# First loads cut into pieces in the order of use, and conditioned weight chunks awaited in halves

## What is computed

```python
w = weight[adapter_ids]
h = jnp.einsum('bsi,boi->bso', x, w)              # the conditioned product

gu_s = x2 @ shared_w_gate_up.T                    # x2 is h, as (2048, 1024)
shared_out = jax.nn.silu(g_s) * u_s @ shared_w_down.T
probs = jax.nn.softmax(x2 @ gate_w.T, axis=-1)
topk_vals, topk_idx = jax.lax.top_k(probs, 2)     # then normalised
gu = jnp.einsum('th,eih->eti', x2, w_gate_up)
out_e = jnp.einsum('eti,ehi->eth', jax.nn.silu(g) * u, w_down)
return x + moe_out + shared_out
```

## Time and profile before

| | |
|---|---|
| median of 3 runs | 1063.91 us (1063.42 to 1065.25) |
| the profiled execution | 1064.86 us, span 1063.1 us |
| TensorE matmul busy | 1055.3 us (99%), 4826 matmuls |
| VectorE busy | 634.1 us (60%) |
| ScalarE busy | 457.0 us (43%) |
| GpSimd busy | 272.8 us (26%) |
| DMA | 248.03 MB, mean 233 GB/s |
| granted TensorE clock | 1.000 over the span |

### The profile page before, as it was taken

The page is one execution under the profiler, slowest core; times in us unless marked ns, Lnnn a source line. Parts: engine busy times, 40 slices in busy tenths (PEclk is TensorE's granted clock), DMA queues, the critical chain, the costliest instruction groups (busy, mean ns, idle before and its releaser), DMA issues.

```text
span 1063.1 us, 15851 instructions
## 1 busy us (share of the span) xinstructions
PE 1055.3 (99%) x4826; PEld 870.8 (82%) x4827; DVE 634.1 (60%) x650; ACT 457.0 (43%) x527; POOL 272.8 (26%) x325
## 2 busy tenths in 40 slices
PE   8999999999999999999999999999999999999998
PEld 7888888888888888887888888888888888888887
DVE  6666765536756667867866867354553545544454
ACT  6565644532223556756655755232223222322310
POOL 1000000000026655555555550121003200033040
PEclk9999999999999999999999999999999999999999
DMA  9899877422256779987987865663566336564355
GB/s 351 325 348 342 315 286 258 190 79 81 88 209 211 263 273 348 335 313 270 352 351 265 291 248 213 246 229 119 145 232 237 138 118 182 194 237 144 113 183 211
DMA packets 55350, 248.03 MB, mean 233 GB/s; under 512 B 8146, under 2 KB 21586, under 8 KB 45394
## 3 DMA queue, kind: packets, MB, share of 16 engines
q1 hardware_dynamic: 29394, 161.50, 42.0%
q0 software_dynamic: 19008, 62.41, 17.0%
q10 hardware_dynamic: 6912, 23.66, 5.9%
HBM read 200.87 MB, written 43.52 MB: 230 GB/s over the span
## 4 chain that ended last, share of the span: by engine, by line
PE 98%; DMA 1%; issue 1%; DVE 0%; ACT 0%; SPq 0%; ACTq 0%; DVEq 0%
PE bank L568 32%; PE bank L570 32%; PE bank L569 32%; PE bank L593 1%; PE bank L779 1%; DMA raw<-cond_w 0%; ACT w_split_sb L863 0%; PE bank L581 0%; PE bank L712 0%; PE bank L602 0%; DVE w_split_sb L1157 0%; DMA ids<-ids 0%; PE bank L699 0%; PE bank L747 0%; DVE rows L1413 0%
## 5 line engine op out<-in xcount | busy, mean ns | idle before, releaser
L1157 DVE TENSOR_TENSOR w_split_sb<-raw,w_split_sb 128x2048 fp32r<-128x2048 f32 (+3 forms) x152 | 257.3, 1724 | 60.0 <-ACT w_split_sb L863 58.8
L863 ACT ACTIVATE w_split_sb<-raw 128x2048 fp32r<-128x2048 f32 (+3 forms) x152 | 215.7, 1456 | 63.7 <-PE bank L570 53.5
L507 POOL DMA_INDIRECT h_in<-h_dram,idx_h x156 | 175.5, 1125 | 122.6 <-DVE tile_f L1462 75.1
L568 PE MATMUL bank<-hT_hi,w_split_sb 128*128 128x512 f32 x512 | 199.7, 390 | 0.0
L569 PE MATMUL bank<-hT_lo,w_split_sb 128*128 128x512 f32 x512 | 199.2, 389 | 0.0
L570 PE MATMUL bank<-hT_hi,w_split_sb 128*128 128x512 f32 x512 | 199.2, 389 | 0.0
L568 PE MATMUL bank<-w_split_sb,tile_hT 128*128 (+1 forms) x312 | 124.8, 400 | 0.0
L570 PE MATMUL bank<-w_split_sb,tile_hT 128*128 (+1 forms) x312 | 122.0, 391 | 0.0
L569 PE MATMUL bank<-w_split_sb,tile_hT 128*128 (+1 forms) x312 | 121.7, 390 | 0.0
L570 PEld LDWEIGHTS bank<-hT_hi,w_split_sb 128*128 128x128 f32 x512 | 96.1, 188 | 20.0
L568 PEld LDWEIGHTS bank<-hT_hi,w_split_sb 128*128 128x128 f32 x512 | 96.1, 188 | 19.9
(11 more groups left out here) (153 smaller groups left out, 1417.0 us busy)
## 6 DMA issues: line engine op xcount, KB each, us to landing
raw<-sh_gu_w SPq DMA_DIRECT2D x16, 2048.0 KB, 9.3
raw<-exp_gu_w SPq DMA_DIRECT2D x16, 2048.0 KB
raw<-cond_w SPq DMA_DIRECT2D x14, 2048.0 KB, 9.8
y_dram<-y_out ACTq DMA_DIRECT2D x39, 512.0 KB
raw<-sh_down_w SPq DMA_DIRECT2D x8, 2048.0 KB, 7.7
raw<-exp_down_w SPq DMA_DIRECT2D x16, 1024.0 KB
h_dram<-h_blk POOLq DMA_DIRECT2D x16, 512.0 KB, 8.8
x_raw_sb<-xT SPq DMA_DIRECT2D x7, 1024.0 KB, 9.6
```

The lines of the kernel that those rows point to most:

```text
L507: nc.gpsimd.indirect_dma_start(out=h_in[par][:, i, :], out_offset=None, in_=h_blocks, in_offset=bass.IndirectOffsetOnAxis(ap=idx_h[par][:, ...
L568: nc.tensor.matmul(dst, lhs[0], rhs[0], start=first, stop=False)
L863: return nc.scalar.activation(dst, src, ACT.Copy)
L1157: return nc.vector.tensor_tensor(dst, src, hi.bitcast(F32), ALU.subtract)
```

## The change

It has these parts.
- ScalarE's queue issues two of the four x pieces at the start, the third after the copy of the first, the fourth after the copy of the first w piece. The gate weights are loaded after the last w piece's copy, and their copy and subtraction stand at unit 4.
- ScalarE and VectorE take one x piece (two k), then its two w pieces, and so on. Each x piece has a signal of its own for TensorE (`first_x_split`).
- TensorE does both token tiles per k of the first chunk (`first_batch`), in banks 2 and 3, then the second chunk's units in banks 0 and 1, awaited by quarters (`second_split`).
- SP loads the third chunk in quarters, each when its part of the raw buffer has been split; ScalarE and VectorE split it, and TensorE awaits it, by quarters.
- TensorE awaits each later conditioned chunk in two halves (`w_begun` ahead of k = 0, `w_split` ahead of k = 4).
- 7 x 9 dummy matmuls instead of 8 x 9.

The core of the diff (semaphore declarations, starting values and repeated forms are left out):

```diff
+            def x_load(b):
+                sp.wait_ge(x_split, b + 1)
+                sp.dma_start(x_raw_sb[:, :], xT[bass.ds(b, 1), :, :].rearrange("o p n -> (o p) n")).then_inc(x_in, 16)
+
+            def first_loads():
...
+                x_load(1)
+                a = sp.value_load(small["ids"][0:1, 1:2], min_val=0, max_val=ADAPTERS - 1)
+                for i, landed in enumerate(third_w):
+                    c0, c1 = i * CH // 4, (i + 1) * CH // 4
+                    if i < 3:
+                        sp.wait_ge(first_split, 2 * i + 2)
+                    else:
+                        sp.wait_ge(w_split, 3)
+                    sp.dma_start(raw[0][:, c0:c1], cond_w[bass.ds(a, 1), 0, :, c0:c1].rearrange("o p n -> (o p) n")).then_inc(landed, 16)
+                chunk(3, 1, cond_w[bass.ds(a, 1), 1, :, :].rearrange("o p n -> (o p) n"))
...
+            def first_batch():
+
+                for k in range(KT):
+                    if k == KT - PIECE_K:
+                        pe.wait_ge(x_split, 2)
+                    elif k % PIECE_K == 0:
+                        pe.wait_ge(first_x_split, k // PIECE_K + 1)
+                    if k < KT - 1:
+                        pe.wait_ge(first_split, k + 1)
+                    else:
+                        pe.wait_ge(w_split, 3)
+                    for m in range(2):
+                        last = first_product(bank[2 + m][:, :], 0, m, k)
+                        if k == KT - 1:
+                            last.then_inc(h_mm, 1)
+                for m in range(2):
+                    for k in range(KT):
+                        if m == 0 and k == KT - 2:
+                            pe.wait_ge(w_split, 4)
+                        elif m == 0 and k % 2 == 0:
+                            pe.wait_ge(second_split, k // 2 + 1)
+                        last = first_product(bank[m][:, :], 1, m, k)
+                    last.then_inc(h_mm, 1)
...
-                        if not first or b2 or n:
-                            pe.wait_ge(w_split, 4 * q + 2 * b2 + n + 3)
+                        third = first and b2 == 1 and n == 0
+                        if not third:
+                            pe.wait_ge(w_begun, 4 * q + 2 * b2 + n - 2)
...
+                                if m == 0 and third and k % 2 == 0 and k < KT - 2:
+                                    pe.wait_ge(third_split, k // 2 + 1)
+                                if m == 0 and k == (KT - 2 if third else KT // 2):
+                                    pe.wait_ge(w_split, 4 * q + 2 * b2 + n + 3)
...
-            with pe.Fori(0, 8):
+            with pe.Fori(0, 7):
...
+            for i in range(2):
+                first_x_load(i)
...
+                if i == 0:
+                    first_x_load(2)
+                for k in (2 * i, 2 * i + 1):
+                    act.wait_ge(first_w[k], 16)
+                    copy(w_split_sb[:, 0, 0, k * HALF:(k + 1) * HALF], raw[0][:, k * HALF:(k + 1) * HALF]).then_inc(first_hi, 1)
+                    if k == 0:
+                        first_x_load(3)
...
+            def w_hi_third():
+                act.wait_ge(h_mm, 4)
+                for i, landed in enumerate(third_w):
+                    act.wait_ge(landed, 16)
+                    copy(w_split_sb[:, 0, 0, i * CH // 4:(i + 1) * CH // 4], raw[0][:, i * CH // 4:(i + 1) * CH // 4]).then_inc(third_hi, 1)
...
+                    if first and u == 1:
+                        x_hi_part(1, 1)
```

More of the change, by code:

```diff
@@ L178, in adaln_ffn_kernel @@
         second_w = [sem(f"second_w{i}") for i in range(4)]
+        third_w = [sem(f"third_w{i}") for i in range(4)]
         second_hi = sem("second_hi")
+        second_split = sem("second_split")
+        third_hi = sem("third_hi")
+        third_split = sem("third_split")
+        w_begun = sem("w_begun")
         first_hi = sem("first_hi")
+        first_x_split = sem("first_x_split")
         first_split = sem("first_split")
@@ L315, in _ @@
             sp.sem_inc(x_in, 16)
-            sp.sem_inc(raw_in[0], 16)
+            sp.sem_inc(raw_in[0], 32)
             sp.sem_inc(raw_in[1], 16)
@@ L336, in cond_loads @@
+            def cond_loads(q):
                 for b2 in range(2):
                     b = 2 * q + b2
[L338 to L346, removed]
@@ L351, in cond_loads @@
                         chunk(4 * q + 2 * b2 + n, n, cond_w[bass.ds(a, 1), n, :, :].rearrange("o p n -> (o p) n"))
-                        if n == 0 and not first:
+                        if n == 0:
                             move(2 * q - 2 + b2, b2)
-            cond_loads(0, first=True)
+            first_loads()
             with sp.Fori(1, QUARTERS) as q:
@@ L604, in transpose_logits, with first_product @@
                 last.then_inc(lt_mm, 1)
+            def first_product(dst, n, m, k):
+                return product(dst, [x_split_sb[0][:, hl, k, m * P:(m + 1) * P] for hl in range(2)],
+                               w_cols(n, k, 0, HALF), k == 0, k == KT - 1)
+            def first_batch():
[20 more added lines that the diff above has]
+                    last.then_inc(h_mm, 1)
             def cond_quarter(q, first=False, ends=False):
                 for b2 in range(2):
-                    if not first or b2:
-                        pe.wait_ge(x_split, 2 * q + b2 + 2)
+                    if first and b2 == 0:
+                        first_batch()
+                        continue
+                    pe.wait_ge(x_split, 2 * q + b2 + 2)
                     for n in range(2):
-                        if not first or b2 or n:
-                            pe.wait_ge(w_split, 4 * q + 2 * b2 + n + 3)
+                        third = first and b2 == 1 and n == 0
+                        if not third:
+                            pe.wait_ge(w_begun, 4 * q + 2 * b2 + n - 2)
                         for m in range(2):
@@ L849, in _, with first_x_load @@
         def _(act):
-            for i in range(PIECES):
+            def first_x_load(i):
                 act.dma_start(x_raw_sb[:, i * PIECE_K * SEQ:(i + 1) * PIECE_K * SEQ],
                               xT[0, :, i * PIECE_K * SEQ:(i + 1) * PIECE_K * SEQ]).then_inc(first_x[i], 16)
-            act.dma_start(small["gate_raw"][:, :, :], gate_w).then_inc(gate_in, 16)
-            act.sem_inc(w_hi, 4)
+            for i in range(2):
+                first_x_load(i)
+            act.sem_inc(w_hi, 6)
             act.sem_inc(x_hi, 1)
@@ L916, in cond_quarter @@
                         w_hi_second()
+                    elif first and u == 2:
+                        w_hi_third()
                     elif m == 0:
@@ L920, in cond_quarter @@
                             w_hi_half(c, (n + 1) % 2, hf, (h_mm, 2 * c, 16 * (2 * q + b2 + (1 if n == 0 else 2))))
-                    if n == 0 and m == 1 and not (last and b2 == 1):
+                    if n == 0 and m == 1 and not (last and b2 == 1) and not (first and b2 == 0):
                         act.wait_ge(h_mm, UPQ * q + 4 * b2 + 2)
                         x_hi_part(2 * q + b2 + 1, 1 - b2)
+                    if first and u == 4:
+                        gate_hi()
                     if u == 6 and last:
```

69 lines of the change are left out of this document (37 added, 32 removed).

## The result

| | kernel before | changed kernel |
|---|---|---|
| median (lowest to highest, 22 runs each) | 1063.96 us (1063.05 to 1065.82) | 1062.68 us (1062.13 to 1063.46) |
| ratio, 95% interval | | 0.9988 (0.9982 to 0.9993) |
| the profiled execution, span | 1064.86, 1063.1 us | 1062.65, 1060.7 us |

The change makes the kernel faster by 1.28 us, 0.12% (0.07% to 0.18%). The forecast was 2.87 us to 1061.0; the range, 1060.2 to 1062.8, holds the measured median close to its upper end, and by the bound of 0.2% the outcome is "no change", which had a chance of 0.27 against 0.68. So the direction was right, the size less than half. The question is where 1.6 us went.

A forecast was written before the change was run, and what follows sets the result against it. TensorE bounds the kernel, so only its idle time can move: 1.93 us from the earlier start plus 0.94 us of later waits make 2.87 us, from 1063.91 to 1061.0 us, with a range of 1060.2 to 1062.8 us.

The forecast's parts named there:

- What bounds the kernel, and the work after the front: TensorE, busy 1055.3 of 1063.1 us, bounds the kernel; its work stays, so only its 7.8 us of idle time can move.
- The start: First real matmul at 8.12 instead of 10.05, as less data travels ahead of w piece 0: 1.93 us gained.
- I add 0.2 and take 6.6: Landing time of w piece 0, with 0.2 us added for the pieces queued behind it that share the engines.
- the prediction's own sign, landing after 7.1: Stated test at the start: the prediction is wrong if w piece 0 lands after 7.1 us.
- Cost: nothing, with 0.5 us of cover at the tightest place: First chunk, both tiles per k: no waits for pieces; tightest is w piece 1, ready at 9.0 and due at 9.5.
- Second and third chunk by quarters: Third and fifth units: quarters are ready before they are due, so TensorE no longer waits; 0.94 us lost there before.
- covers of 1.8 and 3.1 us: Predicted margins between quarters being ready and due: 1.8 us for the second chunk, 3.1 us for the third.
- Waits by halves, dummies, gate weights: Later chunks' added waits, already met, and the moved gate load cost nothing; nine fewer dummies end near 7.85, not 8.26.
- A: At the start, w piece 0 shares engines with the third x piece: gain only 1.8 us, 1062.1 us; chance 0.13.
- B: Gain given back behind 30 us, as late third-chunk copies hold unit 4: 1062.1 to 1062.6 us; chance 0.10.
- C: At the start, w piece 0 comes no earlier, its 5.3 us being its own latency: 1063.0 us; chance 0.04.
- D: Every added wait in the middle of a product costs 0.27 us, met or not: slower, 1066.9 us; chance 0.05.

The follow-up runs named there:

- c0: The changed kernel once more, with no edit, as control; 0.9987 of the kernel before, medians 1063.52 and 1064.82 us.
- e2: Changed kernel with x pieces 2 and 3 issued by SP, after w pieces 3 and 5, instead of by ScalarE; 0.9985 of the kernel before, median 1062.87 us.
- e7: Changed kernel with the first chunk again one token tile after the other, piece waits in the first tile only; 1.0018 of the kernel before, 1065.98 us.
- e10: Changed kernel with the third chunk loaded in one 2 MB load and awaited whole before unit 4; 1.0035 of the kernel before, median 1067.53 us.
- e11: Changed kernel with the late x pieces on SP and 8 x 9 dummies; 0.9981 of the kernel before, medians 1062.15 and 1064.14 us.
- e5: Changed kernel with 8 x 9 dummy matmuls, as in the kernel before, instead of 7 x 9; 0.9989 of the kernel before, median 1063.04 us.
- e3: Changed kernel with the 13 later conditioned chunks awaited whole instead of in halves; 0.9993 of the kernel before.
- e4: Changed kernel with w pieces 2 to 7 issued as three 512 KB loads instead of six of 256 KB; 1.0002 of the kernel before.
- e8: Changed kernel with three x pieces at the start, the fourth by SP after w piece 5, and 8 x 9 dummies; 0.999 of the kernel before.
- e6: Changed kernel with the second chunk awaited whole before its unit 2 instead of by quarters; 1.0018 of the kernel before, median 1065.91 us.
- e1: Changed kernel with all four x pieces issued at the start on ScalarE's queue; 0.9992 of the kernel before, median 1063.59 us.
- e9: Changed kernel with all four x pieces issued at the start and 8 x 9 dummies; 0.9996 of the kernel before.

## Why the prediction was right or wrong

**What bounds the kernel, and the work after the front: right.** Only the idle time of PE before 38.46 changed. From the sixth unit to the router's matmuls it took 49.12 us in the profiles of the kernel before and of the changed one.

**The start: the estimate for a good execution, taken for all of them.** The step "I add 0.2 and take 6.6" for w piece 0 was met by the profiled run (6.38). Over the ten profiled executions with two x pieces ahead (changed, c0, e2 to e7, e10, e11) the piece landed at 6.4 to 8.2, on average 7.35. Its ninth engine came at 5.9 to 6.6 in each. The rate-based sum described the typical engine. The term that was mis-sized is the 0.2 us added for company: the last engine came 0.3 to 1.8 us after the ninth. By the prediction's own sign, landing after 7.1, it was wrong in six of the ten.

**The first chunk: the step that failed.** "Cost: nothing, with 0.5 us of cover at the tightest place" named k = 1 as the tightest. PE waited there in e5 (0.42 us), e7 and e10, where w piece 1 landed at 8.70, 9.77 and 9.82. Tightest was k = 2: piece 2 had to land by about 9.2 (due at 10.7 in the changed profile, less the 1.5 from landing to matmul), and landed at 9.97 to 11.34 in the changed kernel and its copies with the same loads. The prediction checked ScalarE and VectorE against PE, piece by piece, but not the DMA engines, which it took to be moving bytes as fast as before. They moved 946 KB from 5 to 9 us where they had moved 1237. The effective starts of the four executions with exactly these loads and full use of them (changed 9.39, c0 9.85, e3 9.74, e5 9.24) average 9.56: 1.4 us of the forecast 2.87 went in these two steps, and 10.99 - 9.56 = 1.4 us is left, which is what the medians show (1.28 and 1.30). In the changed kernel, e3 and e5 most or all of it was lost behind the first product (7.91, 8.49, 8.10), in c0 ahead of it (9.55).

Shown of its cause: x piece 2 takes the engines from w piece 2, or 3, and delays w piece 2 by 1.1 to 1.4 us at the ninth engine (e11 and e2 against changed). But taking x piece 2 out of the way did not give the 1.4 us back. The medians of e2 and e11 lie 1.95 and 1.99 us below the kernel before, against 1.13 to 1.30 for the changed kernel, c0, e3 and e5, so it gave back 0.7 us or so, by intervals that overlap, and the two profiled executions start effectively at 9.53 and 9.27, hardly earlier than 9.56. What holds these is the last engine of w piece 0. So the loss has two sources, the turns with x piece 2 and the spread between the engines of one load, and a late piece 0 hides a late piece 2; how they share the 1.4 us isn't measured better than that. Not settled: why the engines, with pieces queued, are idle for a tenth to a third of the time between 4 and 9 us, and which of them come last. It isn't SP's pace (e4) nor simply the number of bytes issued early (e8).

**Second and third chunk by quarters: right in the outcome, on landings that were wrong.** The prediction let the second chunk's first quarter land at 15.1 and the third chunk end at 26.35, as before. In the changed kernel they landed at 16.21 and 27.84, in c0 at 16.86 and 30.13. The covers of 1.8 and 3.1 us, and of 1.9 for the eviction of unit 2, took that up, except in c0. No wait is left at the third unit, and none or 0.27 us at the fifth. Taking either away opens a gap of the size expected from the changed kernel's times (e6: 1.8 expected, 2.37 measured; e10: 1.9 and 1.72). In the sum they stood for 0.94 us, since that was what the kernel before lost there; with an earlier start, and chunks that land later, they are what keeps the rest of the gain.

**Waits by halves, dummies, gate weights: right** at nothing (e3, e5), though the dummies ended at 7.13 in the changed kernel and at 8.68 in e3, not at 7.85. The gate weights had no run of their own.

**The rivals.** A had the right mechanism, at piece 2 or 3 instead of piece 0. That its price (1.1 us of loss) is near the measured 1.4 is luck, since only part of the 1.4 comes from it. Its chance of 0.13 was too low: the prediction dismissed it by arguing that w piece 0 would be in by then, and never asked about the pieces behind it. B was seen once, at 0.27 us. C is out: piece 0 comes earlier than before's 8.53 in every execution with two x pieces ahead. D is out (e3). Slower than before came about only where parts of the change were taken away (e6, e7, e10); there units wait for chunks that land later than before, and in some executions the pause costs clock too. That the range holds the median, 0.12 us inside its upper end, is owed to its having been widened for A and B; the forecast alone reached to 1061.7.

## What to carry to other kernels

When first loads are cut into pieces, compute for every piece when its last DMA engine is due, not only for the first, and use the slowest landing seen, not the mean rate; the first piece's gain is worth only what the second and third allow. Keep loads that are needed in one order on one queue: a piece issued beside them from another engine's queue delays the one that is needed next (here by over 1 us at the ninth engine; in the kernel's time it was likely worth 0.7 us). Parts that remove waits behind an earlier start (both tiles per k, quarters) have to be made with it; without them this kernel, with the same early start, was slower than before (e6, e7).

## What the runs showed of the hardware

- In the first 11 us of an execution the first and the last of the 16 engines of one 256 KB load of w finished 0.8 to 3.6 us apart, and the last up to 2.6 us after the ninth, each time differently.
- A fall of TensorE's granted clock was seen after pauses of 3.48 us (e1), 2.37 us (e6), and 1.84 and 0.69 us close together (e7), in e1 and e6 about 1.3 and 1.5 us after the pause had ended; matmuls of 512 columns then stood 0.43 us apart instead of 0.23 for about 3 us. It was not seen after 2.5 us (c0), 2.2 us (e9), 2.0 us (e8), 1.72 us (e10), 1.6 us (e2) and 1.38 us (changed). A pause near 2.4 us can go either way. Not foreseen: in a kernel with 99% PE time, a pause near 2.4 us can cost more than itself.
- The 256 KB loads on one queue and a 256 KB load on another, under way together: from 6.5 to 7.5 us the one queue moved 0.12 MB and the other 0.20 MB (changed); alone the first moved 0.27 MB (e2).
- The same 63 small matmuls at the start took 4.91 to 6.53 us (c0, e3): 12 to 14 a microsecond at first, 20 to 22 later, the step coming at 5 us in c0 and not before 8 in e3, while the profile shows a granted clock of 1.00 all along.
- A wait that is already met, in the middle of an accumulation, cost nothing that shows (0.22 us step at k = 4, and 13 such waits fewer made e3 no faster).
